# A sandwich block of attention and experts: VectorE norms and other PSUM places at the end, and another order of VectorE and fillers at the start

## What is computed

```python
x = x + _layernorm(attn(_layernorm(x)))      # 16 heads of 8, softmax of q k^T / sqrt(128), then w_out
x = x + _layernorm(ffn(_layernorm(x)))
# ffn, by token:
logits = xf @ Wr + expert_bias; top_v, top_i = top_k(logits, 2)
rw = softmax(top_v) scattered to the 8 experts
h = silu(x Wg[e]) * (x Wu[e]);  out = sum_e rw[e] * (h Wd[e])      # 8 experts of 64
out = out + silu(xf @ Sg) * (xf @ Su) @ Sd                          # shared expert of 128
```

## Time and profile before

| | |
|---|---|
| Median of 3 runs | 373.0 (370.69, 373.0, 379.14) |
| Profiled execution | 370.51 |
| Its span, from the first to the last instruction | 368.7 |
| Mean granted TensorE clock | 0.996 |

### The profile page before, as it was taken

The page is one execution under the profiler, slowest core; times in us unless marked ns, Lnnn a source line. Parts: engine busy times, 40 slices in busy tenths (PEclk is TensorE's granted clock), DMA queues, the critical chain, the costliest instruction groups (busy, mean ns, idle before and its releaser), DMA issues.

```text
span 368.7 us, 10052 instructions
## 1 busy us (share of the span) xinstructions
PE 352.0 (95%) x3304; PEld 228.4 (62%) x3304; DVE 312.6 (85%) x788; ACT 267.5 (73%) x511; POOL 201.1 (55%) x518
## 2 busy tenths in 40 slices
PE   8999999999999999999999999999999999998892
PEld 8857645554565657575757565666765556666772
DVE  8697788989999999999897999999989986767660
ACT  4762678689788878968886788688768878864522
POOL 7333052414654464767574564755773676767654
PEclk9999999999999999999999999999999999999998
DMA  2556876454656565355566554487265141322111
GB/s 84 139 134 145 186 192 123 132 116 130 155 156 131 159 139 138 100 123 163 132 185 164 147 123 123 128 177 177 81 184 133 33 116 38 111 64 71 52 38 31
DMA packets 59922, 45.65 MB, mean 124 GB/s; under 512 B 8966, under 2 KB 56966, under 8 KB 59870
## 3 DMA queue, kind: packets, MB, share of 16 engines
q1 hardware_dynamic: 59870, 45.00, 48.3%
HBM read 26.69 MB, written 17.81 MB: 121 GB/s over the span
## 4 chain that ended last, share of the span: by engine, by line
PE 67%; DVE 9%; issue 9%; POOL 9%; ACT 3%; SPq 1%; DMA 1%; POOLq 0%; DVEq 0%; ACTq 0%
PE pvp L661 12%; PE bank_d L815 8%; PE sc L645 8%; PE bank_d L831 7%; PE sc L629 7%; PE bank_d L816 6%; DVE mx L1010 5%; PE bank_d L668 4%; PE bank_a L714 3%; POOL hidden L1219 2%; POOL rstd L1152 2%; PE bank_d L788 2%; PE bank_d L806 1%; PE sc L610 1%; ACT pr L859 1%
## 5 line engine op out<-in xcount | busy, mean ns | idle before, releaser
L1010 DVE TENSOR_REDUCE mx<-sc 128x4 f32<-128x1024 f32 x128 | 154.2, 1217 | 16.7 <-PE sc L629 16.0
L859 ACT ACTIVATE pr<-sc 128x1024 f32<-128x1024 f32 x128 | 130.8, 1024 | 24.5 <-PE sc L645 23.6
L661 PE MATMUL pvp<-pr,va 128*32 128x256 f32 x1024 | 68.5, 385 | 0.0
L815 PE MATMUL bank_d<-x3T,wg_sb 128*128 128x256 f32 x160 | 54.3, 421 | 2.5 <-DVE hidden L1108 1.9
L645 PE MATMUL sc<-qs,ks 51*128 51x256 bf16 x512 | 49.7, 274 | 1.5 <-DMA qs<-mT 0.9
L629 PE MATMUL sc<-ks,qs 48*128 48x256 bf16 x512 | 49.6, 272 | 1.5 <-DVE mx L1010 1.1
L1219 POOL TENSOR_TENSOR hidden<-hidden,rwb 128x256 f32<-128x256 f32 x60 | 42.3, 731 | 10.1 <-DMA rwb<-rw_dram 10.1
L816 PE MATMUL bank_d<-x3T,wu_sb 128*128 128x256 f32 x160 | 47.6, 379 | 0.0
L1152 POOL TENSOR_TENSOR rstd<-vareps,mhalf 128x2 f32<-128x2 f32 x64 | 44.6, 697 | 0.0
L661 PEld LDWEIGHTS pvp<-pr,va 128*32 128x32 f32 x1024 | 26.7, 109 | 25.1 <-issue 12.4
L942 ACT ACTIVATE th<-bank_d 128x256 f32<-128x256 f32 x80 | 30.5, 382 | 13.7 <-PE bank_d L816 11.7
(11 more groups left out here) (115 smaller groups left out, 530.5 us busy)
## 6 DMA issues: line engine op xcount, KB each, us to landing
rwb<-rw_dram SPq DMA_DIRECT2D x30, 256.0 KB, 4.3
qk_dram<-parts SPq DMA_DIRECT2D x30, 192.0 KB, 2.6
qs<-qk_dram SPq DMA_DIRECT2D x30, 192.0 KB, 4.0
ks<-qk_dram SPq DMA_DIRECT2D x30, 192.0 KB, 4.5
qk_dram<-parts SPq DMA_DIRECT2D x30, 128.0 KB, 2.4
pv_dram<-pv_sb SPq DMA_DIRECT2D x14, 256.0 KB, 2.5
x_sb<-in_L_attn_x_dram SPq DMA_DIRECT2D x16, 128.0 KB, 2.8
out_dram<-x SPq DMA_DIRECT2D x16, 128.0 KB, 1.8
```

What stands on the lines that cost most here:

```text
L661: mm = pe.matmul(pvp[32 * j:32 * j + 32, g, :], values[:, X * c + 4 * g + j, 32 * tt:32 * tt + 32], pr[:, k, c * N:(c + 1) * N], start=(tt ...
L815: pe.matmul(bank_d[bank][:, 0:N], wg_sb[:, ORDER[n], :], x3T[b % 2][:], start=True, stop=True)
L859: nc.scalar.activation(pr[:, 2 * s:2 * s + 2, :].rearrange("p k n -> p (k n)"), sc[PAIR["s2", b, s]][:].rearrange("p u c n -> p (u c n)"), ...
L1010: nc.vector.tensor_reduce(mx[b % 2][:, :, :, s].rearrange("p c u -> p u c"), sc[PAIR["s1", b, s]][:], AX.X, ALU.max).then_inc(max_done, 1)
```

## The change

**Start.** Batch 0's norm 1 is applied by VectorE (`apply_here`: subtract the mean, multiply by rstd), and GpSimdE makes only the rstd for it (`root`: two operations). VectorE's layout copies `lay0a` and `lay0b` go from ticks 56 and 84 behind the statistics of batch 1 (117, 118), ScalarE's `lay1` from 72 to 121, `wqk` from 100 to 81 and the apply from 96 to 82. `wv` goes from 136 to 153, GpSimdE's `minusm` from 104 to 189 (behind `part3`), `v` of batch 0 from 176 to 193 (behind `sel2`, 192), `va1` from 200 to 237 (behind `ql_copy`, 236). The fillers in front of the first `xT` fall from 17 to 8.

**End.** From batch 14 on the chunks rotate over three banks, `bank_a` with the two `bank_d`. `down` of batch 13 goes to `pvp`, that of batch 14 to `sc[1]`, that of batch 15 by halves to `pvp` and `sc[1]`; x3T and logits of batch 15 go to `sc[0]`. Norms 2 and 3 of batch 15 and norm 4 of batches 14 and 15 use `root` and are applied by VectorE, which also makes their adds. Batch 15's norm 4, last add and store are done by halves, and `down` of 14 and 15 wait for their products one by one. The fillers in front of `gu4` of batch 14, of the router of batch 15, and of the last `down` (6) are gone. Ticks that move, with batch 14's order on TensorE then being `gu0`, `gu1`, `gu2`, `down` of batch 13, `x3T` of batch 15, `gu3`, `gu4`: `gu2` of 14 from 7280 to 7256, `down` of 13 from 7376 to 7260, `x3T` of 15 from 7404 to 7262, `gu4` of 14 from 7344 to 7320 and of 15 from 7568 to 7520 (in front of `wsel`, 7532). On GpSimdE the weights of batch 14 go from 7336 to 7290 (in front of the fourth `hw` of batch 13, 7296) and those of 15 from 7500 to 7470; `rstd4` of 13 from 7472 to 7565 and `add4` of 13 from 7520 to 7566. On VectorE norm 2 of batch 15 has its apply at 7275, its add at 7276, `wT` of 14 goes from 7364 to 7281, norm 3's statistics and apply are at 7280 to 7290, the first `ha` and `hb` of 14 at 7285 and 7286. On ScalarE `tanh4` of 14 (7372) and the x3T copy of 15 (7408) keep their places.

```diff
-    "lay0a": [56],
+    "lay0a": [117],
...
-    "minusm": [104],
+    "minusm": [189],
...
-    "va1": [200],
+    "va1": [237],
...
-    "s2_4": {0: 3}, "s2_5": {0: 4}, "sel1": {0: 3}, "xT": {0: 17, 3: 4, 5: 1},
+    "s2_4": {0: 3}, "s2_5": {0: 4}, "sel1": {0: 3}, "xT": {0: 8, 3: 4, 5: 1},
...
 FILL_LAST = {
-    "down": {15: 6},
-    "gu4": {14: 1},
-    "router": {14: 1, 15: 1},
+    "router": {14: 1},
 }
...
+    ROOTS = [(1, 0), (2, LAST), (3, LAST), (4, LAST - 1), (4, LAST)]
...
+        FREE = LAST - 1
+        banks = [bank_d[0], bank_d[1], bank_a]
+
+        def bank_of(b, n):
+            return (1, 0, 2)[(CHUNKS * (b - FREE) + n) % 3] if b >= FREE else BANK[n]
...
+        down_at = {LAST - 2: pvp[:, 0, :], LAST - 1: sc[1][:, 0, 0, :]}
+        last_down_at = [pvp[:, 0, 0:P], sc[1][:, 1, 0, 0:P]]
+        last_x3T_at = sc[0][:, 1, 0, :]
+        last_router_at = sc[0][:, 1, 1, :]
...
                 if (b := due(tick, "down")) is not None:
...
-                    turn(d_empty[0])
+                    if b < LAST - 2:
+                        turn(d_empty[0])
+                        d_empty[0] = (down_copied, b + 1)
+                    if b == LAST:
+                        pe.wait_ge(down_copied, LAST - 1)
                     pe.wait_ge(h_done, CHUNKS * (b + 1))
+                    if b < LAST - 1:
+                        pe.wait_ge(hw_done, 4 * (b + 1))
+                    for c in range(TT):
+                        dst = last_down_at[c] if b == LAST else down_at.get(b, bank_d[0])[:, c * P:(c + 1) * P]
+                        for n in ORDER:
+                            if c == 0 and n < 4 and b == LAST - 1:
+                                pe.wait_ge(hw_done, 4 * b + n + 1)
+                            if c == 0 and n < 4 and b == LAST:
+                                pe.wait_ge(last_hw_done, n + 1)
...
+                        if b == LAST:
+                            mm.then_inc(last_down_done, 1)
...
+            def apply_here(L, b, t, dst, src, done):
+                p = b % 2
+                nc.vector.tensor_scalar(dst, src, mv[L][p][:, t, 0:1], rstd[L][p][:, t:t + 1], ALU.subtract, ALU.mult).then_inc(done, 1)
+
+            def last_moments(t):
+                p = LAST % 2
+                dve.wait_ge(last_down_done, t + 1)
...
+                nc.vector.bn_stats(st[4][p][:, t, :], last_down_at[t]).then_inc(stats_done[4], 1)
...
+                nc.vector.bn_aggr(mv[4][p][:, t, :], st[4][p][:, t, :]).then_inc(aggr_done[4], 1)
+
+            def last_apply(b, t):
+                p = b % 2
+                src = last_down_at[t] if b == LAST else down_at[b][:, t * P:(t + 1) * P]
+                dve.wait_ge(root_done, ROOTS.index((4, b)) + 1 + (t if b == LAST else 0))
+                dve.wait_ge(add4_done, b - 1)
+                apply_here(4, b, t, y4[p][:, t, :], src, last_applied)
+                dve.wait_ge(last_applied, TT * (b - LAST + 1) + t + 1)
+                dve.wait_ge(stored[p], landed(1, b - 2))
+                nc.vector.tensor_tensor(x4[p][:, t, :], y4[p][:, t, :], x2[b % X2_RING][:, t, :], ALU.add).then_inc(last_add_done, 1)
...
+                if due(tick, "apply1") == 0:
+                    dve.wait_ge(root_done, 1)
+                    for t in range(TT):
+                        apply_here(1, 0, t, xn[0][:, t, :], x_sb[0][:, t, :], applied[1])
...
+                if (b := due(tick, "stats4")) == LAST:
+                    last_moments(0)
+                    last_apply(LAST - 1, 0)
+                    last_apply(LAST - 1, 1)
+                    last_moments(1)
...
+                if (b := due(tick, "aggr4")) == LAST:
+                    for t in range(TT):
+                        last_apply(LAST, t)
...
+            def root(L, b, t=slice(0, TT)):
+                p = b % 2
+                pool.wait_ge(aggr_done[L], TT * b + (t.stop if L == 4 else TT))
...
+                nc.gpsimd.tensor_tensor(vareps[L][p][:, t], mv[L][p][:, t, 1], eps[:, t], ALU.add).then_inc(root_begun, 1)
+                begun[0] += 1
+                pool.wait_ge(root_begun, begun[0])
+                nc.gpsimd.tensor_tensor(rstd[L][p][:, t], vareps[L][p][:, t], mhalf[:, t], ALU.pow).then_inc(root_done, 1)
...
+                if (b := due(tick, "store")) == LAST:
+                    for t in range(TT):
+                        sp.wait_ge(last_add_done, TT + t + 1)
+                        sp.dma_start(out[LAST, t * P:(t + 1) * P, :], x4[LAST % 2][:, t, :]).then_inc(last_stored, DMA)
```

More of the change, by code:

```diff
@@ L812, in _ @@
                         pe.wait_ge(x3T_copied, b + 1)
-                        bank = BANK[n]
-                        turn(d_empty[bank])
-                        pe.matmul(bank_d[bank][:, 0:N], wg_sb[:, ORDER[n], :], x3T[b % 2][:], start=True, stop=True)
-                        pe.matmul(bank_d[bank][:, N:2 * N], wu_sb[:, ORDER[n], :], x3T[b % 2][:], start=True, stop=True).then_inc(gu_done, 1)
-                        d_empty[bank] = (h_done, CHUNKS * b + n + 1)
+                        bank = bank_of(b, n)
+                        dst = banks[bank]
+                        turn(a_empty if bank == 2 else d_empty[bank])
+                        pe.matmul(dst[:, 0:N], wg_sb[:, ORDER[n], :], x3T[b % 2][:], start=True, stop=True)
+                        pe.matmul(dst[:, N:2 * N], wu_sb[:, ORDER[n], :], x3T[b % 2][:], start=True, stop=True).then_inc(gu_done, 1)
+                        if bank == 2:
+                            a_empty = (h_done, CHUNKS * b + n + 1)
+                        else:
+                            d_empty[bank] = (h_done, CHUNKS * b + n + 1)
                 if (b := due(tick, "down")) is not None:
@@ L866, in _ @@
                     nc.scalar.copy(mT[b % 2][:], bank_a[0:3 * H, 0:N]).then_inc(max_copied, 1)
-                if (b := due(tick, "apply1")) is not None:
+                if (b := due(tick, "apply1")) is not None and b:
                     act.wait_ge(x_load[b % 4], DMA * (b // 4 + 1))
@@ L918, in _ @@
                     nc.scalar.copy(flat(proj[b % 2]), bank_d[0][:, 0:N]).then_inc(proj_copied, 1)
-                if (b := due(tick, "apply2")) is not None:
+                if (b := due(tick, "apply2")) is not None and b < LAST:
                     if b >= 2:
@@ L922, in _ @@
                     apply(2, b, y2[b % 2], proj[b % 2])
-                if (b := due(tick, "apply3")) is not None:
+                if (b := due(tick, "apply3")) is not None and b < LAST:
                     if b >= 2:
@@ L930, in _ @@
                         act.wait_ge(gu_done, CHUNKS * (b - 1))
[L931 removed]
+                    nc.scalar.copy(x3T[b % 2][:], last_x3T_at if b == LAST else bank_d[1][:, 0:N]).then_inc(x3T_copied, 1)
                 if (b := due(tick, "ge")) is not None:
@@ L946, in _ @@
                         act.wait_ge(applied[4], TT * (b - 1))
-                    nc.scalar.copy(flat(down[b % 2]), bank_d[0][:, 0:N]).then_inc(down_copied, 1)
-                if (b := due(tick, "apply4")) is not None:
+                    nc.scalar.copy(flat(down[b % 2]), down_at.get(b, bank_d[0][:, 0:N])).then_inc(down_copied, 1)
+                if (b := due(tick, "apply4")) is not None and b < LAST - 1:
                     if b >= 2:
@@ L1065, in _ @@
                     aggr(3, b)
+                if due(tick, "apply3") == LAST:
+                    dve.wait_ge(root_done, ROOTS.index((3, LAST)) + 1)
+                    dve.wait_ge(x3T_done, LAST - 1)
+                    for t in range(TT):
+                        apply_here(3, LAST, t, x3[LAST % 2][:, t, :], x2[LAST % X2_RING][:, t, :], applied[3])
                 if (b := due(tick, "lg")) is not None:
@@ L1159, in _ @@
                     if (b := due(tick, f"rstd{L}")) is not None:
-                        moments(L, b)
+                        if (L, b) == (4, LAST) and (L, b) in ROOTS:
+                            for t in range(TT):
+                                root(L, b, slice(t, t + 1))
+                        elif (L, b) in ROOTS:
+                            root(L, b)
+                        else:
+                            moments(L, b)
                 if (b := due(tick, "part3")) is not None:
@@ L1190, in _ @@
                     nc.gpsimd.tensor_tensor(on[b % ON_RING][:], oc[b % 2][:], rden[b % 2][:], ALU.mult).then_inc(norm_done, 1)
-                if (b := due(tick, "add2")) is not None:
+                if (b := due(tick, "add2")) is not None and b < LAST:
                     pool.wait_ge(applied[2], TT * (b + 1))
@@ L1221, in _ @@
                                                 rwb[b % 2][:, :, n].rearrange("p g t r -> p t g r"), ALU.mult).then_inc(hw_done, 1)
-                if (b := due(tick, "add4")) is not None:
+                if (b := due(tick, "add4")) is not None and b < LAST - 1:
                     pool.wait_ge(applied[4], TT * (b + 1))
```

124 lines of the change are left out of this document (78 added, 46 removed), and 34 rows, old and new, of the table TIMES.

## The result

| | before | changed |
|---|---|---|
| median of 9 runs each, us | 371.5 (370.69 to 379.14) | 369.3 (367.34 to 371.53) |
| profiled execution, us | 370.51 (span 368.7) | 370.93 (span 369.1) |
| TensorE's granted clock, mean | 0.996 | 0.996 |

The ratio is 0.9942, 95% interval 0.9914 to 0.997: 0.6% faster, 2.2 us where 4.8 were forecast. Timed again, the changed kernel had a median of 370.3 (366.69 to 374.58, 12 runs) beside 371.15, ratio 1.0008 (0.9975 to 1.0041). Three of all executions in this document ran at a lower granted clock (0.982 to 0.986) and are left out of the ratios: 373.98 and 374.58 of the changed kernel timed again, whose median without them is 369.61, and 376.61 of the start alone (372.38 without it).

What follows compares the result with a forecast made beforehand. TensorE, busy 95% of the span, was taken as the bound, so only its idle or unneeded work could go. Start 1.0 plus end 3.8 took 4.8 off 370.5, giving 365.7; 1.0 added for a median made 366.7, range 363.0 to 371.5.

Steps and rivals of the forecast that it cites:

- my two ends: VectorE's two applies for batch 0: ending at 5.6, or at 6.5 if GpSimdE's work beside them gets in the way.
- If the pace still rises near 7.2: Start: if TensorE's pace rises as before despite the filler break, `part1` comes at 8.4 against 10.36, 1.95 earlier.
- Rival A: Start: TensorE's low pace lasts longer because fillers break; first maximum 0.9 later than before, 368.6 us; chance 0.20.
- so 0.45 is given back: Start: with `v` behind `sel2`, the second transpose waits for its copy in the same bank, so `sel3` ends 1.5 earlier.
- Start: 1.0 saved: First maximum at 18.0, not 18.91, then VectorE bounds four maxima; range from 2.0 saved to 0.9 lost.
- So 1.5 us of TensorE is idle here: End: `down` of batch 13 waits for GpSimdE's fourth product, which ends at 342.1, after TensorE finishes three chunks at 340.6.
- the copy can't start before 346.95, as against 347.00: End: batch 15's x3T copy stands behind batch 14's `tanh4`, which needs chunk 4, so the router starts when it did before.
- chunk 3 waits 0.45: End, batch 15: chunk 3 waits 0.45 for chunk 0's bank; `down` of batch 14 then starts at 354.7 against 355.96.
- End: 2.7 + 1.1 = 3.8: Last `down` ends at 359.35 against 362.06, 2.7 saved; tail 5.5 against 6.65, 1.1 saved; range 2.3 to 5.5.
- Rival C: End: the forecast waits are too long; 2.7 of 4.0 idle is absent, gain 7.5, 364.0 us; chance 0.12.
- Rival B: End gives only fillers 1.34 and tail 1.1, since `down` 13's place costs what the third bank saves; 368.1 us; chance 0.13.
- Rival D: Start: low pace lasts to the end of `sel3`, first maximum 4.6 later than before; slower, 372.3 us; chance 0.05.

Runs made afterwards that it cites:

- the start alone: The kernel before with only the change's start (moved stages, 8 fillers, VectorE's applies) and the old end: 372.59 us, ratio 1.0016.
- the end alone: The kernel before with only the change's end (third bank, moved downs, VectorE's last norms, no last fillers) and the old start: 367.48 us, ratio 0.9879.
- the experiment on the weights: The changed kernel with `va1` back and GpSimdE's fourth product of batch 13 ahead of batch 14's weights (7297 for 7290): 368.66 us, ratio 0.9935.

## Why the prediction was wrong

The direction was right and the time within the range, but the gain was less than half of what was forecast. By its steps:

- *"so xT starts at 6.0 instead of 1.52 + 6.93 = 8.45"*: 6.0 was right, 5.88. The two applies took 0.76 beside `pick`'s select, where two others in SBUF took 0.60 (those of norm 2 of the last batch): between my two ends, near the shorter. But 8.45 is the value of one execution of the kernel before, whose rise was at 7.57. In the end alone, with the same fillers and the rise at 4.97, the transposes start at 7.14.
- *"If the pace still rises near 7.2 ... `part1` at 8.4"*: 8.42 in the second profile of the same kernel, 7.86 to 8.23 in the six other profiles with 8 fillers, 9.20 in the first. The condition was the right one, and it does not hold every time. Rival A is what the first profiled execution shows; its price up to `part1` was put at 0.8 and was 0.8. The rise came at any time between 4.38 and 11.04, late in one of the eight profiles with 8 fillers. The Trainium skill ("TensorE: Matmul & The Clock Gate", Part 1) has the moment vary from run to run; the runs agree that it varies, and by more than the half microsecond either way that the page gives: with the same fillers from 1.52 on it came at 4.97, 7.31 and 7.57.
- *"so 0.45 is given back"* (`v` behind `sel2`): 0.3 to 0.4 up to `ql_copy`, but 0.86 up to `rest1`. The size was right only for the first.
- *"`rest1` of batch 1 0.69 to 18.0, and the first maximum starts at 18.0"*: 18.10 in the second profile, 17.91 in the start alone. The operations were placed well. Then came the step that failed: ***"From there VectorE is the bound for four maxima. Start: 1.0 saved."*** I followed `rest1` only to the maximum that stands behind it on VectorE, and put what it feeds at nothing. It starts the trip through DRAM of batch 1's q and k. In the old start that trip had 0.4 to 0.5 to spare in three profiles, and the scores followed the first maximum by 13.10. In all nine profiles with the new start its landing ends last, and the scores follow by 13.27 (second profile) to 14.60 (start alone). On that trip `va1` costs 1.2 and `v` 0.86, and the one long issue of the spill up to 1.5 more than the others. The start's worth at the scores of batch 1 is then 0.64 in the second profile (31.37 against 32.01, with the rise at 7.53 and 7.57), a loss of 1.2 in the one with the late rise, a loss of 1.6 in the start alone against the end alone (rises 4.98 and 4.97), and in the medians nothing (1.0016 for the start alone). How much of the loss in the medians is `va1`, the long issue or the late rise stays open.
- *"So 1.5 us of TensorE is idle here, which no view of before shows"*: 1.50. *"the copy can't start before 346.95, as against 347.00"*: behind `tanh4`, right. *"chunk 3 waits 0.45"*: 0.99, mis-sized by 0.5; it waits for `hidden` of chunk 0, which stands on VectorE behind a reciprocal of the gates that has to wait for GpSimdE. `down` 14 is therefore 0.8 earlier, counted from the last exponential, and not 1.3, and the last matmul ends 2.1 earlier and not 2.7. The tail, forecast at 5.5, is 5.3, with the queue on VectorE as described, and 4.8 without a part of it. *"End: 2.7 + 1.1 = 3.8"*: 3.4 in the first profile, 3.4 in the second, 2.9 in the end alone; the median of the end alone gave 4.1, and the rest of that is not accounted for.
- Rival C (the 1.5 goes and helps) fell with the experiment on the weights; Rival B was wrong about the tail and the third bank. Rival D did not occur in any profile.
- *Sum:* 4.8 was forecast; with the start at 0.64 and the end at 3.4, less 0.2 in the middle, it is 3.8, and that is the second profiled execution (366.69 against 370.51). The medians gave 2.2 and 1.5. The rest is what a single profile cannot show: executions with a late rise, and the waits of the middle. That the time fell into the stated range is no merit of the start's arithmetic: the end gave what was forecast, and the range was wide enough for a start that gives nothing. How often each loss occurs, and whether the changed kernel has more of them than the end alone (six runs within 1.8 us, beside nine within 4.2 and ten within 5.0, on other occasions), stays open.

## What to carry to other kernels

When a stage is moved, follow what it feeds through the DMAs to the instruction of TensorE that needs it, and not only the queue of the engine that it stands in: a memset put ahead of a short operation costs its full length on the trip through DRAM that this operation starts, and the trip may be what ends last although it was not before. Where two chains end within 0.5 us of each other, as here, shortening one gives no more than that. And a gain that is counted from one profile of the kernel before holds for executions like that one: here the moment of the rise alone moved the old start by 1.1 us. Where two parts of a change touch different ends, time them apart: here one of them gave everything, and the version that only mends that one (366.53) is as fast as the best of both. An idle gap on TensorE need not pay when it is closed: here `down` 13 came 1.0 earlier and `down` 14 did not move.

## What the runs showed of the hardware

- Executions differ in when TensorE's pace rises: 4.38 to 11.04 us after the start in twelve profiles, and 7.53 and 11.04 in two of one program, with the fillers' spacing going from 0.21 to 0.11. The rows print a granted clock of 1.00 before the first clock record too, so the count or the spacing of like instructions has to be read there.
- The granted clock can fall in the middle of a busy kernel: with TensorE busy for 1.27 of 4 us it was 0.50 for some 3 us behind it (197.6 to 201.0 in the profile with the weights later), in a stretch that cost 3.0 us.
- One of the six issues of the spill of batch 1 held SyncE's queue for 0.7 to 1.9 us, where most others took 0.4 to 0.5: 0.71 to 1.00 in the three profiles with the old start, 0.68, 0.70, 0.85 and 1.67 in the four with the new start and `va1` behind `ql_copy`, 1.28 to 1.94 in the five with `va1` back. The cause was not tried.
- The last stack of batch 1 landed 5.4 to 6.1 us after its issue in all twelve profiles, although the load of batch 0 landed 2.3 after its issue.
